# Dynamic convolution, two layer norms and a quantised product as one woven stage, with 25 taps in 7 products

## The chip, the cores and the metric

The kernel runs on one core of a Trainium2 chip. The core has a matrix engine (TensorE, PE in the rows; its weight loads are PEld), a vector engine (VectorE, DVE), a scalar engine (ScalarE, ACT), GpSimd (POOL) and SyncE (SP), which here only issues transfers. Each engine takes its own instructions in order and waits on semaphores for the others. The metric is the device time of one execution in microseconds (us). It is the median of three runs.

## The reference, cut to what matters

The program is a network of four layers on an image `x` of 2 x 128 channels x 48 x 48. Layer 0 is a convolution with local attention and a mixture of experts, layer 1 attention and a mixture, layer 2 a dynamic convolution and a quantised product, layer 3 a pruned convolution and a mixture. The part that is changed is all of layer 2 and the norm at the head of layer 3:

```
x = x + L2_conv(_ln_c(x))          # dynamic convolution
t = _to_tokens(x)
t = t + L2_ffn(_ln_t(t))           # quantised product
x = _from_tokens(t, x)
x = x + L3_conv(_ln_c(x))          # begins with the norm "ln6"; the rest is the stage "pruned"

def L2_conv(x):                    # cw: 128 channels to 32
    f = relu(cw @ x + conv_b)
    g = relu(cw @ mean(x over H, W) + conv_b)
    gk, gk2 = per-image, per-channel 5x5 and 3x3 kernels made from g
    y1 = depthwise 5x5 convolution of f with gk, + adap_bias
    y2 = depthwise 3x3 convolution of f with gk2, dilation 2, + atrous_bias
    return fuse_w @ concat(y1, y2) + fuse_b          # 64 channels to 128

def L2_ffn(x):
    w = sign(weight - mean(weight)) - weight + weight, times mean(|weight|)
    y = x @ w + bias
    q = round(clip(y, -1, 1) * 7) / 7
    return y + (q - y)
```

The means that feed `g` go over a whole image. Every norm here is over the 128 channels of one pixel, so a norm of some rows needs only these rows.

## The kernel before

The state `X` [128 channels, 96 rows, 48] stays in SBUF: two images of 48 rows one below the other. A tile `t` is 8 rows or 384 pixels (`T`), so there are 12 tiles (`NT`), six (`TB`) an image. A tile has three chunks of 128 pixels (`CH`). `U` is a second array of this shape and holds a normed `X`.

After the mixture of layer 1, these stages run one after the other, each with a barrier of all engines at its end:

- `layer_norm` "ln4" writes the normed `X` to `U`.
- `dynamic_conv`. `take(t)` turns each product `dc_pre` (32 channels of features, computed four times over on 128 partitions) into four copies in `F`, each shifted by one column: ACT writes two of the four and DVE two. An image of `F` is then split into a rounded part `f_high` (ACT, L1785) and a rest `f_low` (DVE, L1836), since the fp32r products need both. `make_filters(b)` makes 10 filters of 128x128 for an image: four columns of the 5x5 window share one product, the fifth column needs five more. A tile `convolve(t)` is 10 filters x 3 products of 384 columns (L1754), summed in one PSUM bank, and DVE adds it to `X` (L1844). Both splits and the filters of the second image are made between the images.
- `layer_norm` "ln5", `X` to `U`. All 12 tiles are turned (three PE transposes each), copied by ACT (L215) and measured by DVE (`bn_stats`, L241); then one chain of small DVE instructions makes scale and shift of all 36 chunks; then DVE norms two chunks of each tile (L260) and ACT one (L226), PE turns them back and ACT stores them (L231).
- `quantised`. A product per tile, ACT adds the bias (`qf_y`, L1929), and DVE takes six steps on it (L1949, L1958, L1960 with one array operand, L1962, L1964, L1966 with two). Two tiles go in step.
- `layer_norm` "ln6", `X` to the padded image `XP`.
- `pruned`, then the mixture "m7" of layer 3.

What sets the order inside a stage is written out by hand. Some stages (the mixture, and the two attention stages with which one is woven) use `Programs`: each engine has several generators that yield due times, and the one with the smallest due time issues next. The times only give the order; the semaphores alone hold an engine back.

The weights of the last mixture, `in_3` (2048 KB) and `out_3` (1024 KB), are loaded by SP during the mixture "m3" of layer 1 (L1346).

## Time and profile before

| | us |
|---|---|
| median of 3 runs | 1815.44 (1813.77 to 1815.87) |
| the profiled execution, its own time | 1810.06 |
| its span, first to last instruction | 1808.2 |
| dynamic_conv, ln5, quantised and ln6, from first start to the start of `pruned` | 191.45 (from 1292.00 to 1483.45) |
| `pruned` | 57.55 (to 1541.00) |

The span is what lies between the first and the last recorded instruction; 1.9 us lie around it. Positions in rows are us from its start. The changed part is a tenth of it. Over the span PE is busy for 1436.5 us, DVE 981.8, ACT 782.7 and POOL 521.8.

### The profile page before, as it was taken

To read this page: it belongs to the slowest core of one execution; us is meant where nothing else is said; L and a number is where in the kernel's file an instruction comes from. 1 tells how busy PE (TensorE), PEld (TensorE's weight loads), DVE (VectorE), ACT (ScalarE), POOL (GpSimd) and SP (SyncE) were. 2 spreads that over 40 slices of the span, in tenths; PEclk is the share of its full clock that TensorE was granted. 3 is DMA by queue.
4 is the path that set the end of the run, shared out by engine and by line. 5 is a ranking of instruction groups with operands and counts; after the bars stand their busy time and mean duration, and the time that the engine had idled before them with its cause. 6 is when DMAs were issued, how large, how long until landed. Compare 5 with 4: busy or idle time off the path is not lost. (4 is left out here: it accounts for less than half of the span.)

```text
span 1808.2 us, 32545 instructions
## 1 busy us (share of the span) xinstructions
PE 1436.5 (79%) x10176; PEld 1319.5 (73%) x10176; DVE 981.8 (54%) x2723; ACT 782.7 (43%) x2082; POOL 521.8 (29%) x691
## 2 busy tenths in 40 slices
PE   3899989999948999457999987984587568369991
PEld 2899989999947999335999977984377334258880
DVE  7555557886435345356556663432733687654562
ACT  4211234443338777254444454752622443444440
POOL 2300037674133555400000021334000000446655
PEclk7899999999968999778999998997688779679995
DMA  7000001112113543100000001431000000024442
GB/s 253 15 1 1 4 13 27 27 27 83 51 44 109 170 107 101 50 8 1 1 0 1 1 17 34 148 91 53 0 1 0 1 1 0 28 78 122 130 116 73
DMA packets 101758, 89.90 MB, mean 50 GB/s; under 512 B 12360, under 2 KB 93908, under 8 KB 100704
## 3 DMA queue, kind: packets, MB, share of 16 engines
q1 hardware_dynamic: 90080, 64.28, 11.7%
q0 software_dynamic: 11520, 23.62, 4.4%
q8 instruction: 87, 1.43, 0.3%
q14 instruction: 71, 0.58, 0.1%
HBM read 46.43 MB, written 36.70 MB: 46 GB/s over the span
## 5 line engine op out<-in xcount | busy, mean ns | idle before, releaser
L1281 POOL DMA_INDIRECT slots<-U,m_slot_at x180 | 176.4, 980 | 530.3 <-DVE m_slot_at L1196 364.6
L1022 PE MATMUL m_pre<-m_xg,m_own 128*128 128x128 f32 x1888 | 258.4, 281 | 22.3 <-ACT m_h L1112 11.1
L1022 PEld LDWEIGHTS m_pre<-m_xg,m_own 128*128 128x128 f32 x1888 | 237.2, 197 | 27.0 <-issue 24.6
L1112 ACT ACTIVATE m_h<-m_pre,m_own 128x128 f32<-128x128 f32 x572 | 164.4, 378 | 61.6 <-PE m_pre L1022 53.8
L1538 PE MATMUL at_mixed<-at_v,at_probs 128*128 128x130 f32 x1296 | 178.2, 276 | 3.1 <-DVE at_normed L1636 2.3
L1538 PEld LDWEIGHTS at_mixed<-at_v,at_probs 128*128 128x128 f32 x1296 | 173.4, 192 | 7.7 <-ACT at_probs L1600 3.6
L1600 ACT ACTIVATE at_probs<-at_scores 128x384 f32<-128x384 f32 x216 | 105.2, 491 | 146.3 <-PE at_scores L1554 144.6
L1613 DVE TENSOR_REDUCE at_peaks<-at_sampled 128x1 f32<-128x512 f32 (+1 forms) x180 | 112.9, 636 | 59.3 <-PE at_sampled L1521 58.7
L1290 POOL DMA_INDIRECT U<-results,m_slot_at x108 | 103.9, 962 | 131.0 <-DMA results<-m_y 66.6
L1034 PE MATMUL m_out<-out_a,m_h 128*128 x744 | 100.5, 279 | 0.5 <-issue 0.5
L1049 PE MATMUL m_turned<-params_sb,U 128*128 128x128 f32 x108 | 23.0, 333 | 91.0 <-DVE U L1266 67.9
L1034 PEld LDWEIGHTS m_out<-out_a,m_h 128*128 128x128 f32 x744 | 92.2, 195 | 1.0 <-issue 0.8
L694 ACT ACTIVATE l_probs<-l_scores 126x384 f32<-126x384 f32 x96 | 47.2, 491 | 104.3 <-PE l_scores L573 104.3
L573 PE MATMUL l_scores<-l_queries,l_keys 128*126 128x192 f32 x576 | 91.5, 277 | 0.0
L1554 PE MATMUL at_scores<-at_staged,at_k 112*128 112x384 f32 x216 | 80.4, 373 | 10.7 <-DVE at_staged L1626 7.5
L1521 PE MATMUL at_sampled<-at_k,at_staged 112*128 112x512 f32 (+1 forms) x180 | 80.6, 454 | 7.5 <-DVE at_peaks L1613 7.5
L1049 PEld LDWEIGHTS m_turned<-params_sb,U 128*128 128x128 f32 x108 | 15.0, 169 | 95.6 <-issue 95.6
L546 PE MATMUL l_mixed<-high,wqkv_high 128*128 128x384 f32 x216 | 75.5, 349 | 10.7 <-PEq L132 10.7
L1290 POOL DMA_INDIRECT m_others<-results,m_slot_at x72 | 69.3, 963 | 43.5 <-PE m_pre L1022 29.1
L573 PEld LDWEIGHTS l_scores<-l_queries,l_keys 128*126 128x126 f32 x576 | 80.3, 193 | 0.0
L599 PE MATMUL l_mixed<-l_columns,l_probs 126*96 126x65 f32 x768 | 79.0, 246 | 0.0
L546 PE MATMUL l_mixed<-high,wqkv_low 128*128 128x384 f32 x216 | 78.4, 363 | 0.0
(354 smaller groups left out, 3506.4 us busy)
## 6 DMA issues: line engine op xcount, KB each, us to landing
m_x_in<-slots SPq DMA_DIRECT2D x62, 256.0 KB
results<-m_y SPq DMA_DIRECT2D x62, 256.0 KB
slots<-zeros SPq DMA_DIRECT2D x3, 2048.0 KB, 13.2
l_queries<-l_parts SPq DMA_DIRECT2D x256, 18.0 KB, 1.8
slots<-U,m_slot_at POOLq DMA_INDIRECT x180
X<-in_x SPq DMA_DIRECT2D x4, 576.0 KB, 5.5
out<-X SPq DMA_DIRECT2D x12, 192.0 KB
in_a<-in_w SPq DMA_DIRECT2D x1, 2064.0 KB, 8.1
```

What stands on the lines that cost most here:

```text
L546: done = pe.matmul(rows48(conv[c][:, 0:T]), w[:, tap, c * C:(c + 1) * C], x[:, row:row + TR, tap % 3:tap % 3 + W], start=k == 0, stop=k == ...
L573: last = pe.matmul(target, keys[n % HELD][:, lk, g, :], of(lq), start=False, stop=i == 2)
L1022: last = pe.matmul(pre[n % 2][:, c * 128:(c + 1) * 128], own[n % RING][:, c * 128:(c + 1) * 128], xg[n % RING][:, :], start=True, stop=True)
L1034: last = pe.matmul(out[n % 2][:, 0:C], h[(n - 2) % HELD][:, c * 128:(c + 1) * 128], w_out[:, ds(e * (HC * C) + c * C, C)], start=c == 0, s ...
L1112: last = act.activation(h[n % HELD][:, c * 128:(c + 1) * 128], pre[n % 2][:, c * 128:(c + 1) * 128], act_func, bias=own[n % RING][:, HID + ...
L1281: pool.indirect_dma_start(slots[b], bass.IndirectOffsetOnAxis(ap=slot_at[b][k][:, n:n + 1], axis=0), tokens[b][:, n, :], None).then_inc(la ...
L1290: pool.indirect_dma_start((tokens[b] if k == 0 else others[b])[:, n, :], None, results[b], bass.IndirectOffsetOnAxis(ap=slot_at[b][k][:, n ...
L1521: pe.matmul(sampled[(u + piece) % 2][:, 0:cols], staged[u][:, c * 128:(c + 1) * 128], k[:, image * KEYS + j * PC:image * KEYS + j * PC + c ...
L1538: last = pe.matmul(mixed[c][:, 0:VC], probs[n % RING][:, c * 128:(c + 1) * 128], v[:, b * KC + n, :], start=n == 0, stop=n == KC - 1)
L1554: pe.matmul(scores[n % SCORES][:, 0:T], k[:, (b * KC + n) * 128:(b * KC + n + 1) * 128], staged[u][:, :], start=True, stop=True).then_inc( ...
L1600: act.activation(probs[n % RING][:, :], scores[n % SCORES][:, 0:T], ACT.Exp).then_inc(exped, 1)
L1613: dve.tensor_reduce(peaks[:, c, j:j + 1], sampled[(u + piece) % 2][:, 0:min(PC, KEYS - j * PC)], AX.X, ALU.max).then_inc(sampled_used, 1)
```

## The change

`dynamic_conv`, `layer_norm` "ln5", `quantised` and `layer_norm` "ln6" become one stage, `convolved_tail`, which uses `Programs` on PE, ACT and DVE. Each tile of the convolution is followed by its norm, product, quantisation and next norm while later tiles are still convolved. The norms are made by groups of tiles, (0,1,2), (3,4,5), (6,7,8), (9,10) and (11), each with a chain of small instructions of its own, so there are ten chains in place of two.

The fifth column of the 5x5 window no longer takes five filters. Its first four rows are stacked on the partitions as a second array, `down_high` and `down_low`: copies of the first 32 partitions of `f_high` and `f_low`, shifted by 0 to 3 rows. They are filter 5 and the last corner is filter 6, so that there are 7 filters. POOL makes the copies by 8 transfers per image of 32 partitions x 48 x 52 fp32 (312 KB) each. The arrays hold one image, so those for the second image wait for the last product of the first (`conv_ready`).

ACT writes three of four feature copies in the first image, two in the second. Norms are shared the other way: DVE does one chunk in three, ACT two. The quantiser has one PSUM bank in place of two. `in_3` and `out_3` are allocated after the woven stage, and SP loads them in `pruned`.

The core of the diff; waits between the engines are shown where they are new:

```diff
-    TAPS = 10
+    TAPS = 7
+    GROUPS = ((0, 1, 2), (3, 4, 5), (6, 7, 8), (9, 10), (11,))
+    RING = 6
+    PITCH = 7.5
+    def conv_at(t):
+        return 19.0 + PITCH * t
+    def prepare_at(t):
+        if t < TB:
+            return 0.5 + 1.4 * t
+        return conv_at((t - TB) // 2) - 0.05 + 2.5 * ((t - TB) % 2)
+    for m in range(2):
+        for g, tiles in enumerate(GROUPS):
+            for t in tiles:
+                turn_at[m][t] = conv_at(t) + PITCH + (0.0 if t == NT - 1 else 2.6) if m == 0 else norm_at[0][t] + 9.0
+            stat_at[m][g] = turn_at[m][tiles[-1]] + 2.0
+            for i, t in enumerate(tiles):
+                norm_at[m][t] = max(stat_at[m][g] + 3.0 + 4.0 * i, norm_at[m][t - 1] + 2.5 if t else 0.0)
...
+        def tensor_program(pe):
+            def convolution():
+                for t in range(NT):
+                    yield conv_at(t)
+                    if t % TB == 0:
+                        pe.wait_ge(f_split, t // TB + 1)
+                        pe.wait_ge(filters_split, t // TB + 1)
+                    if t >= 2:
+                        pe.wait_ge(conv_used, t - 1)
+                    products(t, (0, 1, 2, 3), 0, 5)
+                    yield conv_at(t) + 2.5
+                    products(t, (4, 6), 0, 5)
+                    if t % TB == 0:
+                        pe.wait_ge(moved, 16 * 8 * (t // TB + 1))
+                    products(t, (5,), 0, 5).then_inc(conv_ready, 1)
+            def turns(m):
+                for t in range(NT):
+                    yield turn_at[m][t]
+                    pe.wait_ge((conv_used, ffn_added)[m], t + 1)
...
+            def backs(m):
+                for t in range(NT):
+                    yield norm_at[m][t] + 1.5
...
+            return Programs(features(), convolution(), quantiser(), turns(0), backs(0), turns(1), backs(1))
...
+            return Programs(features(), make_filters(), signs(), outputs(), *[program(m) for m in range(2) for program in (rows_in, roots, normalise, rows_out)])
...
+            def quantise():
+                for t in range(NT):
+                    u, done = t % 2, t // 2 * 5
+                    for k in range(6):
+                        yield product_at(t) + 1.5 + 0.6 * k
...
+            return Programs(features(), make_filters(), convolved(), constants(), quantise(), norm(0), normalise(0), norm(1), normalise(1))
 
             @block.gpsimd
             def _(pool):
...
                 clear_padding(pool, padded.XP)
+                for b in range(B):
+                    for n, (target, source, ready) in enumerate(((down_high, f_high, f_rounded), (down_low, f_low, f_split))):
+                        pool.wait_ge(ready, b + 1)
+                        if b > 0 and n == 0:
+                            pool.wait_ge(conv_ready, TB)
+                        for j in range(4):
+                            pool.dma_start(target[j * CM:(j + 1) * CM, :, :], source[0:CM, b * PF + j:b * PF + j + H, :]).then_inc(moved, 16)
+                pool.wait_ge(moved, 16 * 8 * B)
...
-def pruned(nc, P, X, padded):
+def pruned(nc, P, X, padded, loads):
...
+            @block.sync
+            def _(sp):
+                for target, source, arrived in loads:
+                    sp.dma_start(target, source).then_inc(arrived, 16)
...
-        dynamic_conv(nc, P, U, X, padded)
-        layer_norm(nc, P, "ln5", X, 1e-5, lambda t: tile(U, t))
-        quantised(nc, P, U, X)
-        layer_norm(nc, P, "ln6", X, 1e-6, lambda t: padded.XP[:, t // TB * PW + 1 + t % TB * TR:t // TB * PW + 1 + t % TB * TR + TR, 1:1 + W])
-        pruned(nc, P, X, padded)
+        convolved_tail(nc, P, U, X, padded)
+        in_3, out_3 = (ctx.enter_context(nc.sbuf_tensor(n, [128, width], F32, side="right")) for n, width in (("in_3", OUT), ("out_3", OUT // 2)))
+        pruned(nc, P, X, padded, [(in_3[:, :], w13_3, loaded_3), (out_3[:, :], w2_3, loaded_3)])
```

## Rows read from the trace of the kernel before

**Rows 1.** Windows: length, busy us of each engine (instructions), granted clock, DMA share, GB/s

```profile
1292.00:1318.80 26.80, 8.66 (x18) 4.37 (x19) 23.68 (x46) 15.12 (x26) 1.98 (x14) 0.63 0.00 1
1318.80:1404.20 85.40, 71.58 (x372) 69.36 (x372) 25.29 (x54) 15.09 (x26) 0.00 (x0) 0.90 0.00 1
1404.20:1426.00 21.80, 13.04 (x72) 9.06 (x72) 15.39 (x68) 16.12 (x38) 0.00 (x0) 0.84 0.00 1
1426.00:1461.00 35.00, 14.21 (x26) 6.07 (x26) 28.98 (x79) 8.02 (x14) 0.00 (x0) 0.72 0.00 0
1461.00:1483.45 22.45, 15.54 (x72) 10.68 (x72) 15.73 (x68) 16.66 (x38) 0.00 (x0) 0.75 0.00 1
```

**Rows 2.** Timeline, start of `dynamic_conv`: start, length, engine, line, out<-in

```profile
1294.71 2.38 ACT L1778 ACTIVATE dc_f<-dc_pre,params_sb 32x384 f32<-32x384 f32 x4 [1.41 <-PE dc_pre L1743]
...
1305.72 0.49 DVE L1861 SCALAR_TENSOR_TENSOR dc_kernel<-params_sb,dc_g 128x10 f32<-128x10 f32 x2
```

**Rows 3.** Groups of instructions by line and shape, `dynamic_conv`: busy us, mean ns | idle before

```profile
L1794 ACT ACTIVATE dc_filters_high<-dc_filters 128x1280 fp32r<-128x1280 f32 x2 | 2.5, 1270 | 5.4 <-DVE dc_filters L1830 5.4
L1844 DVE SCALAR_TENSOR_TENSOR X<-dc_conv,dc_bias,X 128x384 f32<-128x384 f32 x12 | 7.4, 618 | 27.9 <-PE dc_conv L1754 27.7
L1821 DVE TENSOR_SCALAR dc_f<-dc_pre,params_sb 32x376 f32<-32x376 f32 x12 | 7.4, 619 | 0.2
L1836 DVE TENSOR_TENSOR dc_f_low<-dc_f,dc_f_high 128x2704 fp32r<-128x2704 f32 x2 | 6.0, 2976 | 2.0 <-ACT dc_f_high L1785 1.9
L1830 DVE SCALAR_TENSOR_TENSOR dc_filters<-params_sb,dc_kernel,dc_second_part 128x128 f32<-128x128 f32 x20 | 5.4, 346 | 0.0
L1840 DVE TENSOR_TENSOR dc_filters_low<-dc_filters,dc_filters_high 128x1280 fp32r<-128x1280 f32 x2 | 3.0, 1493 | 2.7 <-ACT dc_filters_high L1794 2.7
```

**Rows 4.** The same view of `quantised`, DVE: a step with one array, one with two

```profile
L1949 DVE TENSOR_SCALAR qf_level<-qf_y 128x384 f32<-128x384 f32 x12 | 3.9, 357 | 4.3 <-ACT qf_y L1929 3.6
...
L1964 DVE TENSOR_TENSOR qf_level<-qf_level,qf_y 128x384 f32<-128x384 f32 x12 | 6.1, 553 | 0.0
```

**Rows 5.** The same view of the norm "ln5", DVE

```profile
L241 DVE BATCH_NORM_STATS2 ln_stats<-ln_rows 128x6 f32<-128x128 f32 x36 | 7.1, 289 | 2.6 <-ACT ln_rows L215 2.6
L260 DVE TENSOR_SCALAR ln_normed<-ln_rows,ln_scale,ln_shift 128x128 f32<-128x128 f32 x24 | 6.5, 349 | 0.5 <-PE ln_back L207 0.3 <-DVE ln_shift L253 0.2
```

**Rows 6.** Timeline, a chain of ten small DVE steps in the last mixture, first and last

```profile
1547.01 0.18 DVE L1138 TENSOR_TENSOR m_total<-m_stats 128x12 f32<-128x12 f32 x1
...
1549.06 0.17 DVE L1158 SCALAR_TENSOR_TENSOR m_shift<-m_total,m_scale 128x12 f32<-128x12 f32 x1
```

**Rows 7.** Timeline, products of the convolution at full clock, two steps apart

```profile
1323.08 0.34 PE L1754 MATMUL dc_conv<-dc_f_high,dc_filters_high 128*128 128x384 f32 x1
...
1323.44 0.34 PE L1754 MATMUL dc_conv<-dc_f_high,dc_filters_low 128*128 128x384 f32 x1
```

**Rows 8.** Timeline, the woven output convolution of layer 0, one tile of 27 products

```profile
458.62 0.86 PE L991 MATMUL l_mixed<-judge,X 128*128 128x136 f32 x6
...
458.82 0.62 DVE L781 SCALAR_TENSOR_TENSOR X<-l_scores,params_sb,X 128x384 f32<-128x384 f32 x1 [3.66 <-PE l_scores L621]
459.51 0.51 ACT L1062 ACTIVATE m_rows<-l_mixed 128x408 f32<-128x408 f32 x1 [5.07 <-PE l_mixed L991]
460.06 0.68 DVE L1133 BATCH_NORM_STATS2 m_stats<-m_rows 128x6 f32<-128x128 f32 x3 [0.62 <-ACT m_rows L1062]
464.42 0.62 DVE L781 SCALAR_TENSOR_TENSOR X<-l_scores,params_sb,X 128x384 f32<-128x384 f32 x1 [3.68 <-PE l_scores L621]
```

**Rows 9.** View of the tile `slots`: indirect transfers issued by POOL, ns min/median/max

```profile
L1281 POOL DMA_INDIRECT slots<-U,m_slot_at x180: 956/962/1207, 485.5 to 1677.3; - x180
```

**Rows 10.** Transfers by line: KB each, median us from issue to landing

```profile
slots<-zeros SPq DMA_DIRECT2D x3, 2048.0 KB, 13.2
...
in_a<-in_w SPq DMA_DIRECT2D x1, 2064.0 KB, 8.1
```

**Rows 11.** Windows: the start of the last mixture's experts

```profile
1585.00:1620.00 35.00, 22.21 (x155) 20.87 (x156) 19.28 (x76) 16.70 (x49) 13.39 (x15) 0.76 0.24 72
```

More of the change, by code:

```diff
@@ new lines, in convolved_tail @@
+        norms = [Norm(rows=s.sb(f"rows{m}", [128, RING * CH, C]), stats=s.sb(f"stats{m}", [128, NC, 6]),
+                      normed=[s.sb(f"normed{m}{u}", [128, CH, C]) for u in range(2)], turned=s.ps(f"turned{m}"), back=s.ps(f"back{m}"),
+                      scale=s.sb(f"scale{m}", [128, NC]), shift=s.sb(f"shift{m}", [128, NC]),
+                      small=[s.sb(f"{n}{m}", [128, NC]) for n in ("total", "apart", "squared", "var", "moved", "inv_var")]) for m in range(2)]
+        bias_ps, g_ps, totals_ps = norms[1].turned, norms[1].back, norms[0].turned
@@ new lines, in turns @@
+            def turns(m):
+                for t in range(NT):
+                    yield turn_at[m][t]
+                    pe.wait_ge((conv_used, ffn_added)[m], t + 1)
+                    if t == 0 and m == 0:
+                        pe.wait_ge(weight_ready, 1)
+                    if t >= 1:
+                        pe.wait_ge(copied[m], t)
+                    for j in range(CH):
+                        last = pe.transpose(norms[m].turned[:, j * 128:(j + 1) * 128], chunk(X, t * CH + j), P("identity"))
+                    last.then_inc(rows_turned[m], 1)
@@ new lines, in outputs, with rows_in @@
+            def outputs():
+                for t in range(NT):
+                    yield product_at(t) + 1.0
+                    act.wait_ge(product_ready, t + 1)
+                    if t >= 2:
+                        act.wait_ge(rounding[t % 2], t // 2 * 5)
+                    act.activation(y[t % 2][:, :, :], rows48(product[:, 0:T]), ACT.Identity, bias=P("b2f")).then_inc(y_ready, 1)
+            def rows_in(m):
+                for t in range(NT):
+                    yield turn_at[m][t] + 0.5
+                    act.wait_ge(rows_turned[m], t + 1)
+                    if t >= RING:
+                        act.wait_ge(normed_by_dve[m], t - RING + 1)
+                        act.wait_ge(normed_by_act[m], t - RING + 1)
+                    act.activation(norms[m].rows[:, ring(t):ring(t) + CH, :].rearrange("p n c -> p (n c)"), norms[m].turned[:, 0:T], ACT.Copy).then_inc(copied[m], 1)
@@ new lines, in rows_out, with vector_program, features @@
+            def rows_out(m):
+                for t in range(NT):
+                    yield norm_at[m][t] + 2.4
+                    act.wait_ge(turned_back[m], t + 1)
+                    act.activation(out_tile(m, t), rows48(norms[m].back[:, 0:T]), ACT.Copy).then_inc(stored[m], 1)
+            return Programs(features(), make_filters(), signs(), outputs(), *[program(m) for m in range(2) for program in (rows_in, roots, normalise, rows_out)])
+        def vector_program(dve):
+            def features():
+                link = Chain(dve, step)
+                yield 0.0
@@ new lines, in normalise @@
+            def normalise(m):
+                for t in range(NT):
+                    yield norm_at[m][t]
+                    dve.wait_ge(scale_ready[m], group_of[t] + 1)
+                    if t >= 2:
+                        dve.wait_ge(turned_back[m], t - 1)
+                    for j in by_dve:
+                        n = t * CH + j
+                        last = dve.tensor_scalar(norms[m].normed[t % 2][:, j, :], norms[m].rows[:, ring(t) + j, :],
+                                                 norms[m].scale[:, n:n + 1], norms[m].shift[:, n:n + 1], ALU.mult, ALU.add)
+                    last.then_inc(normed_by_dve[m], 1)
```

429 lines of the change are left out of this document (243 added, 186 removed).

## The prediction

> **What bounds the kernel now.** I read the page first: no engine is full over the span, so a stage must be read by itself. Then the windows, one for each stretch of the changed part [rows 1]. They add up to 191.45 us, and in each another engine works: DVE 23.7 of the first 26.8 us (features, filters), PE 71.6 of the 85.4 us of the convolution, ACT and DVE some 16 each of 22 in either norm, DVE 29.0 of 35.0 in the quantised product. DVE is busy for 25.3 us of the 85.4, and PE for 14.2 of the 35. The reader is to see that the stages don't bound one another by work; the barriers and the all-tiles norms keep them apart. Summed over the five windows, PE has 123 us, DVE 109 and ACT 71.
>
> **The order of the sum.** The change takes work from PE and lets the three engines overlap. I cost the new stage as: time to the first product of the convolution, then DVE's work from there, then the idle time of DVE that cannot be filled.
>
> **To the first product.** Now 26.8 us [rows 1]. ACT starts its copies at 1294.71, four in 2.38 us, 0.59 each [rows 2]. It will do three of four, and `g` comes after 15 of them: 8.8 us, so 1303.5, plus 0.3 for `g` itself. Now the chain that makes the kernels starts at 1305.72 [rows 2]; it would start 1.9 us earlier. After it come `f_low` (3.0, unchanged), and the filters, seven of ten: DVE's 2.7 us an image, ACT's rounding 1.27 and DVE's rest 1.49 [rows 3] shrink by three tenths, 1.6 us. ACT's own six tiles of copies and the rounding of `F` end before the chain does. Sum 26.8 - 3.5, and I take 23.7, since two engines now depend on ACT's slower share; bounds 23 and 26.
>
> **DVE from the first product on.** Twelve additions at 0.618 are 7.4; the second image's features, 12 copies at 0.619, 7.4 [rows 3]. `f_low` 3.0, seven filters 1.9 and their rest 1.0 for the second image, 5.9 [rows 3]. The constants of the quantiser, of the pruned stage and the nine diagonals are some 25 small instructions at 0.22, 5.5 (an estimate at the step of the chain in [rows 6]). Ten chains of eight: ten steps with one short wait on ACT took 2.2 us [rows 6], so 1.7 without the wait, 17.0 in all where two chains were. `bn_stats` of 24 tiles: 0.20 each packed (7.1 by 36) [rows 5], 14.2, or 0.68 for three that stand alone [rows 8], 16.3. One chunk of each norm in place of two: 24 at 0.27 packed or 0.349 alone [rows 5], 6.5 or 8.4. The six steps of the quantiser: 3 x 0.325 and 3 x 0.51 packed or 3 x 0.357 and 3 x 0.553 alone [rows 4], twelve tiles 30.1 or 32.8. Together 94 packed and 101 alone. Now pairs of tiles hide the wait of a step for the one before it; in the new order one tile goes by itself, but eight other programs fall between its steps. I take 97.
>
> **PE is beside it.** A product at full clock takes 0.18 us from start to start (0.36 for two) [rows 7]. 30 a tile become 21, so 252 products are 45 us where 360 were 65. To these come 12 tiles of quantised product and 6 of features, 0.65 each as two passes of four such halves, 11.7, and 48 sets of three transposes. Six judge products with a weight load each held PE for about 0.6 us in the woven stage of layer 0, the 0.86 of the row less the overlap with the next [rows 8]; half of them is 0.3, and I take 0.4 with a hand-over: 19. PE has 77 us at full clock in the stretch where DVE has 97. The 20 us that the three filters save therefore cost and give nothing by themselves: DVE's work covers them. They would count if PE became the bound. ACT has two chunks of each norm, all copies in and out and the outputs: fewer than 65 us by the same rows' sizes, hidden too.
>
> **What DVE must still wait for.** (a) At the start of the convolution, tile 0 has nothing to give; features and constants fill most of its 5 us at low clock: 4, bounds 1 and 8. (b) The tail. After the last addition the last tile goes through turn, copy, stats, chain, norm, turn back, store, product, bias, six steps, and the first seven again. DVE's part of this is about 8 us (2 x 0.68, two chains of 1.7, six steps 2.7, two norms) [rows 4, 6, 8]; sixteen steps of PE and ACT lie between, at 0.5 to 0.8 each, some 9.5. Work of groups 3 and 4 fills a little of it: 8, bounds 4 and 12. (c) The copies of `down_high` and `down_low`.
>
> **The moved rows.** The trace of before has no such transfer on POOL. An indirect one, of 128 rows, is issued in 0.962 us, at most 1.207 [rows 9]; 2048 KB took 8.1 to 13.2 us [rows 10]. Eight transfers are 2496 KB: 7.7 us of issues, 10 to 16 of transfer at those rates. In the first image `down_high` starts when `F` is rounded, well before the filters are done, and `down_low` 3 us later; 18 products at the low clock and two feature products stand before the wait: 0, bounds 0 and 4. In the second image nothing may start before the last product of tile 5, since the arrays hold one image. All eight then lie on the path to the last three products of tile 6, 11 to 17 us after. In its order PE has until then three sets of transposes, one quantised product and 18 products, 5 us, and it waits for DVE's quantisation of tiles 1 and 2 in between (2 x 2.7). So PE stands for 1 to 12 us, and queued behind it are turns, backs and products, for which ACT and then DVE wait. DVE has its own backlog for part of it: 4, bounds 0 and 10.
>
> **Two rules on this point.** The Trainium skill, SBUF — State Buffer, section "Door 1: The DMA port swizzle", says that partitions 0 to 31 reach only half of the ports, at most 218 GB/s. The second image's copies would then be an estimated 12 us, inside the 10 to 16 of the rows; no transfer of 32 partitions stands in this trace. The same page's section "SBUF: two separate sides" says that VectorE in its two-port mode locks GpSimd out, so that the descriptors of a transfer issued on GpSimd are late. It speaks against this change, whose DVE is nearly full. In rows, the step with one array takes 0.357 us for 384 elements and the one with two 0.553 [rows 4]; were each of eight issues held up by 0.553, they would take 12.1 us in place of 7.7, and the stall would be 4 us more. POOL's slowest issue in before, 1.207 against 0.962, shows at most 0.25 [rows 9].
>
> **The sum.** 23.7 + 97 + 4 + 4 + 8 = 136.7, and 0.7 to the start of `pruned` as now: 137.4 in place of 191.45, a gain of 54.0. The profiled execution took 1810.06 us, so 1756; the median of the runs is 5.4 above it, so 1815.44 - 54 = 1761.4. As a check on the weave itself: in layer 0 tiles planned at 6.2 us came every 5.60 [rows 8], so an order by due times can keep its bounding engine full. This plan puts the first product at 19 and the end near 137, 118 us apart; nine tenths of it is 107, and my 113 lies between.
>
> **The rest at nothing.** The loads of `in_3` and `out_3` move past the SP queue of "m3", where they took two issues, into `pruned`: 57.6 us there cover some 12 to 20 of transfer [rows 10], and the experts that use them start near 1597. Without that cover they would cost up to 20. "m3" may gain up to 1 us. `pruned` gets the same inputs.
>
> **Rivals.** First, the forecast's bounds. Low: 23.7 + 94 + 1 + 0 + 4 + 0.7 = 123.4, gain 68, 1747. High: 23.7 + 101 + 8 + 8 + 12 + 0.7 = 153.4, gain 38, 1777. Chance of this case 0.68.
>
> Second, **PE becomes the bound**, by the granted clock. Where PE was busy for 22 of 35 us its granted clock was 0.76, between its levels 2.4 and 1.2 GHz; in the convolution 0.90, and in `quantised`, 14 of 35, 0.72 [rows 1, 11]. Against it, PE has 77 of about 113 us here and pauses are short. At 0.76 its 77 us are 101, about DVE's 97: in-order waits on both sides then add 10 to 15, 1775. At 0.6 they are 128, plus 12 and 4: 144, stage 168.4, gain 23, 1792. The filters saved would count here. Chance 0.15.
>
> Third, **slower: the shifted copies are cut into rows.** A transfer of 32 x 48 rows of 52 elements may be issued row by row (1536 of 208 bytes) and not as 32 pieces. An indirect issue of 128 rows takes 0.962 us [rows 9], so 1536 rows take 11.5, and eight 92. The first image would wait for some 85 us at tile 0, the second again at tile 6: stage about 137 + 165, less what DVE catches up, some 290, time near 1910. It decides from about 4.5 us an issue: 16 issues then are 72 us, less 16 of cover, which is the gain. The arrays are contiguous along both inner dimensions, which speaks against it. Chance 0.07.
>
> Fourth, **the gain is larger**: DVE packs its steps, the second image's copies are quick, and the stage goes below 122: 1745 and under. Chance 0.10.
>
> **How the numbers follow.** The likeliest time is 1761. A range of 1743 to 1788 takes in the first case, the milder half of the second and a part of the fourth, 0.8. About 0.2% is what a measurement of this kernel can tell from no change, 3.6 us. All cases but the third are faster by more, 0.93 less 0.01 for a stage that ends by chance within it: faster 0.92, same 0.01, slower 0.07.
>
> **What would show it.** Between the first product of the new stage and the start of `pruned` 113 us, DVE busy for over 80% of it up to the tail and PE for about 70%; first product 23 to 24 us after the stage's start; a wait of PE on `moved` only in tile 6, of 1 to 12 us; 16 POOL issues of about 1 us; steps of the quantiser near 0.36 and 0.55; no change of `pruned` and of the last mixture. I am wrong if DVE stands idle in the middle of the stage for over 15 us, if the issues on POOL take several us, or if the granted clock in the stage lies under 0.75.

## The result

The changed kernel took 1800.37 us (median of 4 runs, 1796.09 to 1806.39) beside 1814.61 us for the kernel before (4 runs, 1813.24 to 1815.87): a ratio of 0.992, 95% interval 0.9893 to 0.9948. The direction was right and the size was not: a gain of 14 us where 54 were forecast, and a time outside the forecast's range of 1743 to 1788. Run again on another chip it had a ratio of 0.9898 (0.987 to 0.9926). The two intervals overlap between 0.9893 and 0.9926, a gain of 13 to 19 us.

The chips differ: the median of the kernel before was 1768 to 1771 us in three sets of runs and 1812 to 1815 in the two others. So kernels are compared below by their ratios to the kernel before on the same chip, and by the lengths of stages. The woven stage took 173.08 us on a chip of the slower kind and 173.4 on one of the faster. The old stages (191.45 and 192.40) were profiled on chips of the slower kind only. That they take the same on the others is assumed below; the ratios fit it.

### The profile page after: what moved, and what is told of

Same layout as the page of the kernel before. It is cut to its first block and busy times, and to the rows that moved or that the text cites. A ratio compares the mean times of both kernels' runs of the same rounds, so it can differ in the third digit from the quotient of the medians.

```text
span 1804.6 us, 32267 instructions
## 1 busy us (share of the span) xinstructions
PE 1432.5 (79%) x10068; PEld 1309.8 (73%) x10068; DVE 983.8 (55%) x2751; ACT 792.4 (44%) x2112; POOL 528.4 (29%) x707
## 5 line engine op out<-in xcount | busy, mean ns | idle before, releaser
L1112 ACT ACTIVATE m_h<-m_pre,m_own 128x128 f32<-128x128 f32 x572 | 163.8, 377 | 57.6 <-PE m_pre L1022 54.8
## 6 DMA issues: line engine op xcount, KB each, us to landing
slots<-zeros SPq DMA_DIRECT2D x3, 2048.0 KB, 15.7
```

The lines of the kernel that those rows point to most:

```text
L1112: last = act.activation(h[n % HELD][:, c * 128:(c + 1) * 128], pre[n % 2][:, c * 128:(c + 1) * 128], act_func, bias=own[n % RING][:, HID + ...
```

## The profile after

The windows of the changed kernel; columns as in [rows 1]. The first line is up to the first product, the second up to DVE's last addition of the convolution (1441.28), the third up to `pruned`; then `pruned` and the last mixture.

```profile
1299.07:1324.49 25.42, 11.90 (x20) 5.48 (x21) 18.78 (x38) 18.56 (x32) 6.00 (x22) 0.50 0.26 53
1324.49:1441.28 116.79, 80.72 (x384) 67.80 (x384) 68.13 (x221) 47.16 (x100) 3.94 (x8) 0.86 0.17 33
1441.28:1472.15 30.87, 15.19 (x48) 8.62 (x48) 21.91 (x86) 16.48 (x41) 0.00 (x0) 0.57 0.00 0
1472.15:1533.96 61.81, 50.44 (x132) 27.38 (x132) 43.65 (x54) 15.83 (x22) 0.00 (x0) 0.86 0.13 51
1533.96:1804.60 270.64, 173.99 (x1356) 162.86 (x1356) 136.32 (x456) 104.02 (x342) 140.56 (x144) 0.83 0.31 91
```

The five windows of [rows 1], 191.45 us, are now the first three lines, 173.08. From the first product on, DVE is busy for 68.13 + 21.91 = 90.0 us of 147.66 and idle for 57.6; PE is busy for 95.9 (one window over both lines gives a granted clock of 0.80). No engine is full, as before the change, but without barriers to put it down to. The waits between the first product and the end say what replaced them (total us, times, longest).

```profile
ACT dc_rows L1941 <- PE dc_turned L1864: 48.7, 20, 9.5
DVE dc_stats L2087 <- ACT dc_rows L1941: 36.0, 17, 9.3
...
PE dc_back L1875 <- DVE dc_normed L2112: 17.7, 10, 6.9
PE dc_turned L1864 <- DVE X L2077: 13.2, 11, 2.9
```

They form a loop. DVE stands before a tile's statistics because ACT has not copied the rows, since PE has not turned them; and PE stands for what DVE has not yet normed or added. The timeline of one turn of it, PE, ACT and DVE by time:

```profile
1419.36 0.17 DVE L2092 TENSOR_TENSOR dc_total<-dc_stats 128x9 f32<-128x9 f32 x1
...
1419.78 0.34 PE L1824 MATMUL dc_conv<-dc_f_high,dc_filters_low 128*128 128x384 f32 x1
...
1420.72 0.12 DVE L2092 TENSOR_TENSOR dc_total<-dc_stats 128x9 f32<-128x9 f32 x1
...
1422.03 0.56 DVE L2027 SCALAR_TENSOR_TENSOR X<-dc_conv,dc_bias,X 128x384 f32<-128x384 f32 x1
...
1422.70 0.60 DVE L2112 TENSOR_SCALAR dc_normed<-dc_rows,dc_scale,dc_shift 128x128 f32<-128x128 f32 x2
...
1423.67 0.52 PE L1875 MATMUL dc_back<-params_sb,dc_normed 128*128 128x128 f32 x3 [3.55 <-DVE dc_normed L2112]
...
1424.72 0.50 PE L1824 MATMUL dc_conv<-dc_f_high,dc_filters_high 128*128 128x384 f32 x1
1425.02 0.52 PE L1824 MATMUL dc_conv<-dc_f_low,dc_filters_high 128*128 128x384 f32 x1
...
1427.58 0.84 PE L1864 MATMUL dc_turned<-params_sb,X 128*128 128x128 f32 x3
...
1428.45 0.49 ACT L1941 ACTIVATE dc_rows<-dc_turned 128x384 f32<-128x384 f32 x1 [2.96 <-PE dc_turned L1864]
1428.98 0.68 DVE L2087 BATCH_NORM_STATS2 dc_stats<-dc_rows 128x6 f32<-128x128 f32 x3 [5.68 <-ACT dc_rows L1941]
```

The reader is to see that PE and DVE wait in turn. PE starts the last of 12 products at 1419.78, ends it at 1420.12 and stands 3.55 us for a normed tile, which DVE gives late because two chains (from 1419.36 and 1420.72) and its addition come first. Then DVE is done at 1423.3 and stands 5.68 us: the tile that it added at 1422.03 is turned only behind two `back` sets and nine more products, and those run at a pitch of 0.30 to 0.32 us instead of the 0.18 of [rows 7]. The granted clock of these products was 0.53, near the lower of its two levels, 1.2 GHz. It was still 1.00 in the 12 products before, in the pause and in the two `back` sets after it:

```profile
1423.67:1424.72 1.05, 0.80 (x6) 0.59 (x7) 0.00 (x0) 1.05 (x3) 0.00 (x0) 1.00 0.00 0
1424.72:1427.58 2.86, 2.86 (x13) 2.76 (x12) 0.00 (x0) 0.50 (x2) 0.00 (x0) 0.53 0.00 0
```

Nothing in either queue could be taken out of turn.

Sizes of single steps: groups by form, those that answer to [rows 3], [rows 4] and [rows 5], and the copies.

```profile
L2087 DVE BATCH_NORM_STATS2 dc_stats<-dc_rows 128x6 f32<-128x128 f32 x72 | 16.3, 281 | 36.0 <-ACT dc_rows L1941 36.0
L2112 DVE TENSOR_SCALAR dc_normed<-dc_rows,dc_scale,dc_shift 128x128 f32<-128x128 f32 x24 | 7.8, 339 | 0.6 <-PE dc_back L1875 0.6
L2027 DVE SCALAR_TENSOR_TENSOR X<-dc_conv,dc_bias,X 128x384 f32<-128x384 f32 x12 | 7.2, 596 | 0.4 <-PE dc_conv L1824 0.3
L2075 DVE TENSOR_TENSOR dc_level<-dc_level,dc_y 128x384 f32<-128x384 f32 x12 | 6.6, 553 | 0.2
...
L2065 DVE TENSOR_SCALAR dc_level<-dc_y 128x384 f32<-128x384 f32 x12 | 4.2, 350 | 2.1 <-ACT dc_y L1932 2.1
L2133 POOL DMA_DIRECT2D dc_down_high<-dc_f_high x8 | 4.0, 519 | 66.8 <-PE dc_conv L1824 51.0 <-ACT dc_f_high L1901 15.8
```

The durations were as forecast; the idle time in the first row was not. Last, the second image's copies, by timeline and by the view of transfers (KB each, median us to landing):

```profile
1373.64 1.96 POOL L2133 DMA_DIRECT2D dc_down_high<-dc_f_high  x4 [50.99 <-PE dc_conv L1824]
1375.57 2.02 POOL L2133 DMA_DIRECT2D dc_down_low<-dc_f_low  x4
```

```profile
1388.18 0.69 PE L1824 MATMUL dc_conv<-dc_down_high,dc_filters_high 128*128 128x384 f32 x1 [6.93 <-DMA dc_down_low<-dc_f_low]
```

```profile
dc_down_high<-dc_f_high POOLq DMA_DIRECT2D x8, 312.0 KB, 5.4
dc_down_low<-dc_f_low POOLq DMA_DIRECT2D x8, 312.0 KB, 9.2
```

Eight issues take 4 us, not 7.7, and the transfers end about 14.5 us after the first issue; PE stands for the last 6.93 of it. 2496 KB in 14.5 us are 176 GB/s with start and end. In the middle the rate was 193 to 200 GB/s, with the transfer engines busy throughout:

```profile
1376.00:1379.00 3.00, 2.42 (x15) 2.10 (x13) 2.90 (x9) 0.49 (x1) 1.58 (x4) 1.00 0.94 196
1379.00:1382.00 3.00, 1.60 (x9) 1.29 (x9) 1.24 (x4) 0.49 (x1) 0.00 (x0) 1.00 1.04 200
1382.00:1385.00 3.00, 0.00 (x0) 0.00 (x0) 0.00 (x0) 0.00 (x0) 0.00 (x0) 0.83 0.98 193
```

The Trainium skill, SBUF — State Buffer, section "Door 1: The DMA port swizzle", gives 218 GB/s as the most for partitions 0 to 31; the trace lies below it, which agrees. No run took the same bytes from more partitions, so that the partitions set the rate is not shown.

## The experiments

"Stage" is from the first instruction of the changed part to the first of `pruned`. "Loop" is from the first product to the last addition, "tail" from there to `pruned`, both for woven kernels only. The last two columns are DVE's wait before the statistics and PE's wait for DVE's normed tiles. All in us.

| kernel | ratio (95%) | stage | loop | tail | DVE, statistics | PE, normed |
|---|---|---|---|---|---|---|
| before_again | - | 192.4 | | | | |
| changed, after_again | 0.9898 (0.987 to 0.9926) | 173.4 | 117.5 | 30.9 | 35.7 | 18.9 |
| taps_only | 0.991 (0.9889 to 0.9931) | 174.6 | | | | |
| woven_10 | 0.9955 (0.9938 to 0.9973) | 182.5 | 124.9 | 31.0 | 43.2 | 18.7 |
| own_arrays | 0.9857 (0.9834 to 0.988) | 166.5 | 110.6 | 30.9 | 28.7 | 18.3 |
| late_split | 0.99 (0.9879 to 0.9921) | 173.8 | 118.0 | 30.9 | 39.1 | 11.8 |
| two_backs | 0.9891 (0.9865 to 0.9917) | 173.7 | 117.9 | 30.9 | 36.0 | 19.9 (12.4 and 7.5, by bank) |
| lag | 0.9877 (0.9851 to 0.9903) | 170.8 | 108.0 | 37.8 | 22.1 | 18.1 |
| stats_later | 0.9856 (0.983 to 0.9881) | 168.1 | 107.4 | 35.8 | 7.1 | 8.9 |
| own_stats | 0.9848 (0.9829 to 0.9866) | 161.9 | 101.7 | 35.8 | 6.5 | 9.2 |
| thin_dve | 0.9809 (0.9792 to 0.9826) | 157.7 | 102.9 | 29.4 | 30.1 | 17.8 |
| mid_alone | 0.9819 (0.9792 to 0.9846) | 157.7 | 100.1 | 32.3 | 13.7 | 15.4 |
| turn_mid | 0.9789 (0.9763 to 0.9815) | 153.0 | 96.0 | 32.2 | 13.7 | 15.1 |
| mid_ten | 0.9827 (0.9793 to 0.986) | 161.6 | 102.4 | 32.4 | 12.9 | 11.8 |
| mid_lag | 0.9796 (0.9764 to 0.9828) | 155.3 | 93.2 | 36.6 | 14.5 | 11.3 |

Stages of one kernel differ by about 1 us between profiles (191.45 and 192.4; 173.1 and 173.4), so differences under 1 us are read as none. The ratios go over all runs of a kernel; stages and waits are of one profile each.

### The two halves of the change

The kernel before with only the seven products, stages and barriers left as they were:

```diff
-    TAPS = 10
+    TAPS = 7
+        down_high, down_low = (s.sb(n, [128, H, PF], F32R) for n in ("down_high", "down_low"))
```

(and the packing of kernels, the eight copies on POOL and the wait on `moved`, as in the change).

> The kernel before with one part of the change alone: 7 products with the shifted copies, stages one after the other. In the convolution PE is the bound, so both theories expect 108 fewer fp32r products at 0.18 us, 19 us, and 3 us less for the filters; the copies for the second image (14.5 us in the changed kernel) lie beside the 11 us in which PE waits for the second filters now, and 5 us of products. About 1794 us, some 20 below before. If the copies cost more than that cover, 1798 to 1802.

The changed kernel with ten products in the weave, and so without shifted rows, copies and their wait:

```diff
-    TAPS = 7
+    TAPS = 10
-                        pe.wait_ge(moved, 16 * 8 * (t // TB + 1))
```

> The changed kernel with 10 products and no copies: the weave alone. PE has 20 us more work and the wait for the copies is gone (6.9 us and 4 us of low clock behind it). If DVE's work sets the stage, as I forecast, the 20 us are covered and it takes 1790, 10 less than the changed kernel (1800). If instead a tile's time is a loop through PE, ACT and DVE one after the other, so that PE's products add to it, the 20 us come back in large part: 1800 to 1812, and the granted clock in the stage rises above 0.90.

The filters alone save 17 to 18 us of stage (192.4 or 191.45, to 174.6), where some 20 us were expected, or 13 to 17 if the copies cost more than what covers them; PE waited 1.9 us for the copies between the images. The weave alone saves 9 to 10. In whole times that is 8 us, where "DVE's work sets the stage" had 25 and the loop 3 to 15, and the granted clock up to the last addition was 0.93. That is the loop's case. Both together save 18 to 19. The part that the prediction costed at nothing is worth nearly as much by itself as the whole change, and the weave on top of it is worth 1. Windows of both: the whole stage of taps_only, and woven_10 from its first product.

```profile
1266.27:1440.89 174.62, 103.41 (x452) 81.06 (x453) 106.55 (x309) 68.18 (x137) 9.89 (x30) 0.79 0.15 30
```

```profile
1293.09:1449.02 155.93, 109.25 (x540) 92.00 (x540) 91.40 (x309) 64.47 (x145) 0.00 (x0) 0.86 0.00 1
```

### The stall at tile 6

Arrays for both images, so that the second image's copies can start as soon as `f_high` and `f_low` are made. Two small arrays share their space with others to make room.

```diff
-        down_high, down_low = (s.sb(n, [128, H, PF], F32R) for n in ("down_high", "down_low"))
+        down_high, down_low = (s.sb(n, [128, B * H, PF], F32R) for n in ("down_high", "down_low"))
-                        if b > 0 and n == 0:
-                            pool.wait_ge(conv_ready, TB)
```

> The changed kernel with shifted copies for both images, so that the second image's need not wait for the last product of the first. If the copies' late start costs what PE stood for it, the stage loses 7 us of wait and the slow products after it: 1790, some 10 less than the changed kernel. If the time is given back to other waits (each tile is held by DVE's results anyway), 1797 to 1800.

The stage is 6.9 us shorter, as long as PE's wait was, so the stall was not given back to other waits. The prediction had 4 for it, bounds 0 and 10. It is a minor part of the 36 that were missing. And against woven_10, the same weave in the same order and with no stall at tile 6 either (1.7 us of wait for copies are left, at tile 0), three filters less are worth 155.9 - 141.6 = 14.3 us from the first product on. Of this DVE's smaller filters are 1.3 us of work (91.4 against 90.1); the rest stands beside the 19.4 that 108 products take at 0.18. In this order PE's work is not hidden.

The other way round, the second image's filters and split planned a few us later, so that they are out of the way of tiles 3 to 5:

```diff
-                    yield 14.0 if b == 0 else conv_at(3)
+                    yield 14.0 if b == 0 else conv_at(4) + 1.0
```

(the four other places likewise).

> The changed kernel with the second image's f_low and filters moved behind the first group's norm in the order of ACT and DVE (by one tile, conv_at(4)). In the changed kernel PE stood 6.9 us for the first normed chunk, because DVE had f_low (and its wait for f_high), filters and rest, 8.4 us, ahead of the chain. If such waits in a fixed order set the time, it takes 1794 to 1796, 5 less. If the work is only moved and something else waits for it, 1800.

PE's wait for normed tiles fell by 7, DVE's before the statistics rose by 3, and the stage stayed, where 5 us less were expected if such waits set the time: the lost time moved to other places of the loop.

### Which wait holds the loop

The changed kernel itself, for comparison on the same chip as the next three:

> The changed kernel itself once more, beside the others of this call, so that they can be compared with it on one chip. Its ratio to the kernel before should be 0.992 with 0.003 either way; its woven stage 171 to 175 us.

Ratio and stage were as expected.

A second bank for the tiles that the second norm turns back:

```diff
-                        last = pe.transpose(norms[m].back[:, j * 128:(j + 1) * 128], ...
+                        last = pe.transpose(back_bank(m, t)[:, j * 128:(j + 1) * 128], ...
```

> The changed kernel, but the second norm's turned-back tiles alternate between their own PSUM bank and the one of the features, which is free by then. If the one bank serialises the last three tiles (2.3 us apart in the trace of the changed kernel) the stage's end comes 3 to 5 us earlier; if the tail is set by the chain from the last addition through quantiser and statistics instead, nothing changes (within 1 us).

Nothing: stage 173.7. PE's wait for normed tiles did not fall either: it is divided between the two banks, 12.4 and 7.5 us. My reading of the tail, that one bank serialises the last tiles, fell. The last `back` sets of two_backs come at the same distance of 2.26 to 2.29 us, though the banks alternate. Timeline of PE:

```profile
1430.77 0.90 PE L1881 MATMUL dc_pre<-params_sb,dc_normed 128*128 128x128 f32 x3 [1.55 <-DVE dc_normed L2118]
1433.06 0.87 PE L1881 MATMUL dc_back<-params_sb,dc_normed 128*128 128x128 f32 x3 [1.39 <-DVE dc_normed L2118]
1435.32 0.88 PE L1881 MATMUL dc_pre<-params_sb,dc_normed 128*128 128x128 f32 x3 [1.39 <-issue]
```

ACT sets that distance by its own order, as its timeline in the changed kernel shows: it stores a tile before it norms the next one, so store, two normings (0.86) and PE's turn (0.87) follow one another. That is read from the order of the rows; no run changed it.

```profile
1466.12 0.49 ACT L1965 ACTIVATE XP<-dc_back 128x384 f32<-128x384 f32 x1 [1.01 <-PE dc_back L1875]
1466.50 0.86 ACT L1957 ACTIVATE dc_normed<-dc_rows,dc_shift,dc_scale 128x128 f32<-128x128 f32 x2
```

Norms planned later after their statistics:

```diff
-                turn_at[m][t] = ... else norm_at[0][t] + 9.0
+                turn_at[m][t] = ... else norm_at[0][t] + 12.0
-                norm_at[m][t] = max(stat_at[m][g] + 3.0 + 4.0 * i, ...
+                norm_at[m][t] = max(stat_at[m][g] + 6.0 + 4.0 * i, ...
```

> The changed kernel, but each norm is planned 3 us later after its statistics, and the second norm's turn 3 us later after the first norm. If PE's 17.7 us of waiting before it turns normed tiles back (behind which products and turns are queued) sets the pitch, the middle gets 4 to 8 us shorter, less some 3 us of longer tail: 1 to 5 us faster. If the pitch comes from the statistics' place in DVE's order, the middle stays and the tail costs 3 to 6 us: that much slower.

2.6 us shorter, inside the first expectation, but as the difference of two larger numbers: the loop is 9.5 us shorter and the tail 6.9 longer. The next run puts the first norm's statistics behind the addition of the next tile in DVE's order. The group's chain and norms move with them, by 2.5 us of the plan, and so do ACT's and PE's steps of this norm:

```diff
-            stat_at[m][g] = turn_at[m][tiles[-1]] + 2.0
+            stat_at[m][g] = turn_at[m][tiles[-1]] + (4.5 if m == 0 else 2.0)
...
-                    yield conv_at(t) + 5.5
+                    yield conv_at(t) + 4.2
...
-                        yield turn_at[m][t] + 1.0
+                        yield turn_at[m][t] + (3.5 if m == 0 else 1.0)
```

> The changed kernel, but in DVE's order the first norm's statistics of a tile stand after the convolution's addition of the next tile instead of before it (addition planned at 4.2 instead of 5.5 us after the tile's start, statistics 3.5 instead of 1.0 after the turn, the group's chain and norms 2.5 later). Theory A, in-order waits: DVE stands 36 us before the statistics, for a turn that PE has queued behind 21 products, while an addition whose products are done waits behind it and PE waits for that addition's release. Then the waits before the statistics fall by half, and the stage is 6 to 12 us shorter, ratio 0.985 to 0.989. Theory B, PE's low granted clock and its 96 busy us set the pitch, and DVE only waits where it happens to stand: the waits move to the additions or the quantiser, the stage stays within 2 us. Theory C: later norms make the tail longer, 2 us slower.

The wait before the statistics falls from 35.7 to 7.1 and the stage by 5.3 us. Theory A had 6 to 12. Part of the wait moved, as theory B had it: 17.5 us now stand before the quantiser's first step, and the tail is 4.9 longer, as theory C had it. The two edits that helped so far, own arrays and this one, together:

> The two edits that helped, together: arrays of their own for each image's shifted rows (no transfer between the images' products; 6.9 us of stage by itself) and the first norm's statistics later in DVE's order (5.3 us by itself). If the stall at tile 6 and the waits before the statistics are separate losses, the stage takes 160 to 163 us, ratio 0.980 to 0.984. If the later statistics only filled the time of the stall, it stays at 166 to 168.

161.9 is 11.5 under the changed kernel, where the two had 6.9 and 5.3 by themselves: separate losses, as the first expectation had it (160 to 163).

### Does DVE's work set the pace?

Own arrays, and two of the quantiser's six DVE steps left out (the subtraction of `y` and its addition back), 13.2 us of DVE's work:

```diff
-                    for k in range(6):
+                    for k in (0, 1, 2, 5):
```

> Own arrays, and of the quantiser's six steps on DVE two are left out (the subtraction of y and its addition back, which together only replace level by itself up to rounding): 24 steps of 0.56, 13.4 us of DVE's 90 in the stage. Prediction's view, DVE's work sets the stage: 11 to 14 us shorter than with own arrays alone. Rival, the loop over engines sets it: what counts is only the latency of a tile through the quantiser and the tail, with 2 steps less in each link that waits: 3 to 8 us.

8.8 us less than with own arrays, just above the rival's 3 to 8 and under the 11 to 14 of the prediction's view, while DVE's waits before the statistics stay (30.1 against 28.7). So the work left out on DVE counted for two thirds (8.8 of 13.2) and the products left out on PE, above, for three quarters or somewhat less (14.3 of 19.4, with 1.3 of DVE's work in it). If two engines are both full, the two shares can add to one at most; here they add to more, so work on both engines lies one behind the other for a part of the loop. That holds for the work that was left out; for the rest it is inferred.

### The turn in the middle of the products

Own arrays, and PE turns an added tile between the first 12 products of the next tile and the last 9, not behind all 21. This is two numbers of the plan, one for PE's turn and one for DVE's addition:

```diff
-                turn_at[m][t] = conv_at(t) + PITCH + (0.0 if t == NT - 1 else 2.6) ...
+                turn_at[m][t] = conv_at(t) + PITCH + (0.0 if t == NT - 1 else 2.4) ...
-                    yield conv_at(t) + 5.5
+                    yield conv_at(t) + 4.2
```

> Own arrays, and PE turns the added tile between the first 12 and the last 9 products of the next tile instead of behind all 21; DVE's addition is planned ahead of the statistics. If the statistics come late because their turn is queued behind the products, DVE's wait of 28.7 us before them falls under 15 and the stage is 4 to 8 us shorter than with own arrays alone. If the addition comes too late for the turn, PE stands in the middle of its products instead: within 2 us, or slower.

13.5 us less than with own arrays, above the forecast of 4 to 8, and 20.4 less than the changed kernel; 1775.31 us against 1811.99. DVE's wait before the statistics fell from 28.7 to 13.7, under the 15 expected. Its windows up to the last addition and after, then the same spot of the loop, PE first:

```profile
1318.95:1414.90 95.95, 74.53 (x381) 65.42 (x381) 66.57 (x213) 45.63 (x99) 3.88 (x8) 0.92 0.21 41
1414.90:1447.09 32.19, 14.35 (x52) 8.07 (x52) 23.44 (x94) 16.96 (x43) 0.00 (x0) 0.68 0.00 0
```

```profile
1403.02 0.52 PE L1878 MATMUL dc_back<-params_sb,dc_normed 128*128 128x128 f32 x3 [2.35 <-DVE dc_normed L2115]
...
1404.14 0.49 PE L1867 MATMUL dc_turned<-params_sb,X 128*128 128x128 f32 x3
1404.39 0.42 PE L1827 MATMUL dc_conv<-dc_f_high,dc_filters_high 128*128 128x384 f32 x1
```

```profile
1398.63 0.17 DVE L2095 TENSOR_TENSOR dc_total<-dc_stats 128x9 f32<-128x9 f32 x1
...
1400.00 0.56 DVE L2030 SCALAR_TENSOR_TENSOR X<-dc_conv,dc_bias,X 128x384 f32<-128x384 f32 x1
1400.47 0.16 DVE L2095 TENSOR_TENSOR dc_total<-dc_stats 128x9 f32<-128x9 f32 x1
...
1405.25 0.68 DVE L2090 BATCH_NORM_STATS2 dc_stats<-dc_rows 128x6 f32<-128x128 f32 x3 [2.38 <-ACT dc_rows L1944]
```

PE's wait before `back` is still there, but the turn comes right behind it, DVE stands 2.38 us instead of 5.68, and the nine products run beside DVE's statistics, at 0.18 us and a granted clock of 1.00 here. The second number moved DVE's addition between the two chains, where it stood behind both. The statistics of the tile before (1405.25) still come ahead of the next addition (1406.35), so "ahead of the statistics" in the expectation is not what the edit does. The two numbers were not edited apart, so what each of them gives is not shown.

Three runs more, to see whether this edit needs the own arrays, whether PE's products still count, and whether later norms give more:

> The changed kernel with nothing but the order edited: PE turns the added tile between the first 12 and the last 9 products of the next tile, and DVE's addition is planned at 4.2 instead of 5.5 us. The arrays are shared by the two images, as in the changed kernel. If the order was the failed step of the prediction, the stage is 12 to 15 us shorter than 173.3 without any other edit, 158 to 161, ratio 0.982 to 0.985. If the gain needs the stall at tile 6 gone, it is 5 us or less.

> The weave with ten products of filters instead of seven, without shifted rows and their transfers, in the same edited order. PE has 108 products more, some 19 us at 0.18 each. If PE's work is hidden beside DVE's, as predicted, the stage is as long as with own arrays and seven (153), within 3 us. If the loop over the engines holds PE's products in it, it is 12 to 19 us longer, 165 to 172.

> Own arrays and the edited order, the norms planned 1.5 us later after their statistics and the second image's filters and split a little later. If PE's 15.1 us of waiting before it turns normed tiles back, and DVE's 13.7 before statistics, come from norms planned too early, the stage is 2 to 5 us under 153. If the latency from the last addition to the end, 32 us, only grows by it: 1 to 3 us longer.

**mid_alone** is the changed kernel with those two numbers edited and nothing else: 15.7 us less of stage, just over the 12 to 15 expected and more than any other edit gave by itself, and the ratio goes from 0.9898 to 0.9819. **mid_ten** is the same order with ten products and no copies. It is 3.9 us longer than mid_alone and 8.6 longer than turn_mid, of which 1.9 come before the first product. From the first product on, 108 products of 0.18 us cost 134.86 - 128.14 = 6.7 us where they cost 14.3 in the old order; neither expectation (within 3, or 12 to 19) was met. The three filters bring 2.0 us of DVE's work with them in this pair. **mid_lag**, which also has the edit of late_split, is 2.3 us longer than turn_mid, as its second expectation had it (1 to 3): the loop 2.8 shorter, the tail 4.4 longer. Its window from the first product to `pruned`:

```profile
1290.85:1420.69 129.84, 92.87 (x432) 75.44 (x432) 90.31 (x306) 62.10 (x142) 4.13 (x8) 0.80 0.14 30
```

### The parts outside the stage

The kernel before once more, with its `pruned` in the window shown:

> The kernel before, profiled on the chip of this call, to compare stage by stage. The changed part should take 191.5 us as on the other chip; the open point is whether the stage behind it takes 57.6 us here too (against 59.9 to 61.8 in the kernels changed so far) and whether the part ahead of it ends near 1265 us, as in the changed kernels on this chip.

```profile
1485.62:1546.85 61.23, 49.76 (x132) 27.09 (x132) 43.66 (x54) 15.80 (x22) 0.00 (x0) 0.89 0.00 0
```

`pruned` took 57.6 us in the first profile of before, 61.23 in this one (a single execution, of 1817.56 us), and 61.8 in the changed kernel: the 4 us that it seemed to lose are spread. In taps_only, with nothing loaded in it, it took 59.9. The changed kernel's stage began 7 us later than before (1299.07 against 1292.00). Ahead of it the code is the same but for the two loads, which SP no longer issues in "m3". Their place does not show: on one chip taps_only, which keeps them in "m3", began its stage at 1266.27 and three woven kernels at 1263.18 to 1266.57, and on another chip the kernel before began at 1293.22 and three woven ones at 1294.04 to 1294.63. The profiled execution of the changed kernel was the slowest of its four (1806.39 us). The last mixture is spread as well (267.15 before, 270.64 after; 249.6 to 251.8 in all profiles of the faster sets, taps_only with the early loads among them). Moving the loads alone was not run.

## Why the prediction was off, by its own steps

| term | predicted | measured |
|---|---|---|
| to the first product | 23.7 (23 to 26) | 25.4 |
| DVE's work from there | 97 (94 to 101) | busy for 90.0 |
| DVE idle up to the last addition | 4 + 4 (1 to 16) | 116.79 - 68.13 = 48.7 |
| DVE idle in the tail, with the 0.7 to `pruned` | 8.7 | 30.87 - 21.91 = 9.0 |
| stage | 137.4 | 173.1 |

- **The step that failed** is "What DVE must still wait for". It listed a start, a tail and the copies, and gave the middle no idle time at all; it had 48.7 us in place of 8. 34.7 of them are waits before statistics (36.0 less the 1.3 in the tail), 9.3 of these at tile 6. Its own sign of being wrong, DVE idle in the middle for over 15 us, is what came. The reason given for packing, "eight other programs fall between its steps", counts programs. What matters in an in-order queue is where an instruction stands against the moment its input is due, and that could be read from the plan before a run: statistics due 3.6 us after a tile's start, their turn on PE behind 21 products that take 3.8 us at full clock, then 0.5 of turn and 0.5 of copy, so 4.8 at the earliest, and the addition behind them though its products are done at 3.8. The prediction took the plan's times as met.
- That the order is a cause, and the largest found, is shown by mid_alone: two numbers of the plan, the same instructions, 15.7 of the 35.7 us. PE's busy time for these instructions fell from 94.0 (after_again, granted clock 0.82) to 89.8 (0.84), so up to 4 us of the 15.7 may have come by PE's products running faster. That not all of the missing time is this pair is shown too. Own arrays give 4.7 more (turn_mid, 153.0, near the upper end of the forecast's first case, 153.4). The last 15.6 us down to 137.4 stay open: turn_mid still has 128.14 from the first product, 38 of it without DVE, and what is left in the loop I have not pulled apart.
- **"The 20 us that the three filters save cost and give nothing by themselves"** was wrong. They count for 17 to 18 with the stages apart, for 14.3 in the weave as it is, for 6.7 in the better order. The argument set PE's 77 us (its terms add to 76) beside DVE's 97 as if the two ran freely; they run in a loop.
- **Second rival, PE bound by the clock.** The granted clock from the first product on was 0.80, and 77 us at 0.80 are the 96 measured. Its time for the stage at 0.76, some 151, is still 22 short. Stages do not follow the clock from kernel to kernel: woven_10 has 0.86 and 182.5 us, mid_lag 0.80 and 155.3, turn_mid 0.86 and 153.0. But the sum took PE at full clock and found it busy for 19 us more. If these 19 counted like the products left out (14.3 of 19.4), they would be some 14 us of the 36, an estimate, and not apart from the order, since the clock fell behind long waits. No run held the clock fixed, so its own share is not measured, and this rival is not excluded as a part of the cause.
- **The copies.** The stall was 6.93 us on PE and 6.9 in the stage, inside 0 to 10, above the 4. PE also waited for copies at tile 0, 0.7 us, where the prediction had 0, bounds 0 and 4. The third rival, copies cut into rows, did not occur: issues took 0.494 to 0.567 us. Against the two-sides rule (the Trainium skill, SBUF — State Buffer, section "SBUF: two separate sides") these 16 issues show no hold-up: the longest took 0.07 us more than the shortest, where the prediction had priced 0.553 each. But the rows do not say whether any of DVE's steps beside them ran in the two-port mode (it was busy at 1320.69 and at 1373.64, and four issues took 1.96 us both times), so the rule is not tested.
- **The tail** was right in idle time (9.0 against 8.7) and short in length: 21.9 us of DVE's work lay in it, more than the 8 that its last tile needs.
- **DVE's work** was right in its sizes (0.35 and 0.55 a step, 0.68 for three statistics). By line the steps of this stretch add up to 96 us, near the 97. They are 90.0 of busy time because a step often starts before the end of the one ahead (1422.03 and 0.56 make 1422.59, the next starts at 1422.50). The one term that was too large is the ten chains: 17.0, counted from start to start, against 13.1 busy.
- **The first product** was 1.7 us late, inside 23 to 26. The chain that makes the kernels started 13.9 us after the stage's start (1312.95), as before (13.7), and not 1.9 us earlier.
- **The upper bound** was summed with 23.7 and 8 where the terms' own bounds were 26 and 10; with these it is 157.7, still 15 short.
- The check on layer 0, where such an order kept its bounding engine full (PE busy for 5.60 of 5.60 us a tile against 6.2 planned), did not carry over. No run tried why; what differs is that its tile has 27 products and one short chain around it, and this one has two norms and a quantiser in series behind each tile.

## What to carry to other kernels

Before summing engines' work for a woven stage, follow one tile through all queues with the plan's own numbers and ask at each hand-over what stands ahead of it on the producing engine; where the consumer is queued before the producer can be done, that gap recurs each tile, and the engines take turns. A part that looks hidden beside a busier engine must be tried alone: two savings of 17 and 10 us made 18 to 19 together. Put short hand-over work, such as a turn, in the middle of a long run of products, not behind it, and plan what it waits for, here DVE's addition, early enough. The two together were worth 15.7 us here, nearly as much as the whole change.

## What the runs showed of the hardware

Direct transfers of 312 KB are issued by POOL in 0.49 to 0.57 us each, half of an indirect one. Eight of them, read from 32 partitions, took about 14.5 us from first issue to last landing, and moved 193 to 200 GB/s in the middle. Nine products of 384 columns behind a wait of 3.55 us and two `back` sets ran at 0.32 us from start to start, with a granted clock of 0.53, where they take 0.18 at a clock of 1.00; that made them 1.3 us longer. In turn_mid the products behind a wait of 2.35 us and the same two sets ran at 0.18, with 1.00:

```profile
1404.39:1406.06 1.67, 1.67 (x12) 1.67 (x11) 0.81 (x4) 1.67 (x5) 0.00 (x0) 1.00 0.02 5
```
